# Bias rows of a graph network: four float32 rows, or twelve bf16 rows from an exact split

## The reference

```python
gi = x @ w_ih.T + b_ih
gh = h @ w_hh.T + b_hh
r = sigmoid(i_r + h_r); z = sigmoid(i_z + h_z)
n = tanh(i_n + r * h_n)
return (1.0 - z) * n + z * h
```

## Time and profile before

| | |
|---|---|
| three timed runs, us | 3788.97, 3793.4, 3793.51 (median 3793.4) |
| the profiled execution, us | 3787.5 |
| its span, first to last instruction, us | 3785.9 |
| mean granted TensorE clock | 0.836 |
| busy: PE, PEld | 2916.1 us (77%), 1831.7 us (48%) |
| busy: DVE, ACT, POOL | 2178.6 us (58%), 680.5 us (18%), 1629.3 us (43%) |

### The profile page before, as it was taken

The page is one execution under the profiler, slowest core; times in us unless marked ns, Lnnn a source line. Parts: engine busy times, 40 slices in busy tenths (PEclk is TensorE's granted clock), DMA queues, the critical chain, the costliest instruction groups (busy, mean ns, idle before and its releaser), DMA issues.

```text
span 3785.9 us, 53836 instructions
## 1 busy us (share of the span) xinstructions
PE 2916.1 (77%) x10862; PEld 1831.7 (48%) x10863; DVE 2178.6 (58%) x7167; ACT 680.5 (18%) x1768; POOL 1629.3 (43%) x1961
## 2 busy tenths in 40 slices
PE   2157777757778777777688877877777999999998
PEld 1133434435546444444476766642333666455754
DVE  5856666634443588888788888767775000543002
ACT  0012222200013222222100000015552000452000
POOL 0057777754320477777577777500000222001443
PEclk6578898889999888888677677657788999999999
DMA  2034322247641344443433333403332444003887
GB/s 95 33 77 112 108 101 101 101 129 199 192 125 44 84 106 107 107 106 106 74 99 103 102 103 104 77 2 124 126 126 88 146 139 142 1 1 106 276 268 231
DMA packets 317488, 423.25 MB, mean 112 GB/s; under 512 B 182634, under 2 KB 227888, under 8 KB 317014
## 3 DMA queue, kind: packets, MB, share of 16 engines
q0 software_dynamic: 105264, 324.88, 28.8%
q1 hardware_dynamic: 208024, 92.58, 9.4%
q10 hardware_dynamic: 3982, 3.24, 0.3%
HBM read 312.03 MB, written 112.79 MB: 112 GB/s over the span
## 4 chain that ended last, share of the span: by engine, by line
PE 43%; DVE 17%; DMA 13%; POOL 12%; issue 11%; ACT 2%; SPq 1%; DVEq 1%; POOLq 0%; ACTq 0%
PE PSA L846 14%; POOL G L450 7%; PE PSA L810 7%; DMA tab_m<-G,posi 6%; PE PSA L969 5%; PE PSA L833 5%; POOL tab_m L432 4%; DMA G<-tab_k,srci 4%; DVE S L1524 3%; PE PSA L1024 2%; DMA G<-tab_v,srci 2%; DVE S L1525 1%; DMA G<-tab_m 1%; PE PSA L923 1%; PE PSA L805 1%
## 5 line engine op out<-in xcount | busy, mean ns | idle before, releaser
L468 POOL DMA_DIRECT2D G<-tab_A x375 | 201.4, 538 | 1110.3 <-PE PSA L846 644.8
L432 POOL DMA_INDIRECT tab_m<-G,posi x448 | 436.4, 974 | 353.3 <-DVE G L1268 267.3
L450 POOL DMA_INDIRECT G<-tab_k,srci x448 | 426.2, 951 | 306.0 <-DMA tab_v<-KV 169.8
L450 POOL DMA_INDIRECT G<-tab_v,srci x448 | 439.7, 981 | 165.3 <-issue 96.6
L864 PE MATMUL PSA<-ident,oh 128*128 128x128 f32 x896 | 309.1, 345 | 232.2 <-DVE oh L1237 228.5
L969 PE MATMUL PSA<-work,oh 128*128 128x256 f32 x896 | 418.2, 560 | 46.9 <-DVE work L1452 32.0
L602 ACT COPY ohT<-PSA 128x128 f32<-128x128 f32 x896 | 237.5, 265 | 1062.6 <-PE PSA L864 1039.6
L1237 DVE TENSOR_SCALAR oh<-iota_f,dstl 128x128 f32<-128x128 f32 x1344 | 413.9, 309 | 5.5 <-DVE near L1373 0.5
L873 PE MATMUL PSA<-X,ohT 128*128 x896 | 349.4, 481 | 43.7 <-DVE G L1266 22.6
L923 PE MATMUL PSA<-Q,ohT 128*128 x896 | 365.6, 500 | 15.8 <-ACT ohT L602 8.0
L864 PEld LDWEIGHTS PSA<-ident,oh 128*128 128x128 f32 x896 | 143.8, 160 | 471.8 <-DVE oh L1237 448.0
(11 more groups left out here) (315 smaller groups left out, 4118.5 us busy)
## 6 DMA issues: line engine op xcount, KB each, us to landing
G<-tab_A POOLq DMA_DIRECT2D x375, 320.0 KB
tab_A<-G SPq DMA_DIRECT2D x125, 320.0 KB, 2.1
G<-tab_m SPq DMA_DIRECT2D x224, 129.0 KB, 2.6
G<-tab_m POOLq DMA_DIRECT2D x224, 129.0 KB
WT<-tab_m SPq DMA_DIRECT2D x544, 1.0 KB
rec<-tab_rec SPq DMA_DIRECT2D x448, 6.5 KB
tab_m<-G,posi POOLq DMA_INDIRECT x448
G<-tab_k,srci POOLq DMA_INDIRECT x448
```

Of the source, the lines that this page charges most:

```text
L432: pool.indirect_dma_start(tab_m[0:E, :], bass.IndirectOffsetOnAxis(ap=posi[:, t:t + 1], axis=0), G[:, t % GR, :MW], None, bounds_check=E - ...
L450: pool.indirect_dma_start(G[:, t % GR, :p.w], None, p.table, bass.IndirectOffsetOnAxis(ap=srci[:, t:t + 1], axis=0)).then_inc(p.rows[t % G ...
```

## The change

`brow` and `pick` are no longer tiles of their own; they lie in `oh` and `ohT`, which are free at the start, and the whole of `brow` is cleared by VectorE before `v_set`, for which ScalarE now waits before it loads the biases. After the two counts and a wait for the 22 weight turns, VectorE splits `brow` into three bf16 parts (each the rounded rest of the one before) in `Q`, makes `pick` bf16 and adds a fifth block, ones in rows 0 and 1. SyncE copies the three parts into the twelve rows of `bsplit` and three copies of the pick blocks into `bpick`: six transfers. Every bias product is then one bf16 product over all twelve rows.

```diff
-        brow = sb("brow", [4, 3 * D])
-        pick = sb("pick", [4, 4 * P])
+        bsplit = sb("bsplit", [12, 3 * D], BF16)
+        bpick = sb("bpick", [12, 5 * P], BF16)
+        bpart = Q[0:4, 0:3 * (3 * D) // 2].bitcast(BF16).rearrange("p (k n) -> p k n", k=3)
+        brest = Q[0:4, 2048:2048 + 3 * D]
+        bcast = Q[0:4, 4096:4096 + 5 * P // 2].bitcast(BF16)
...
+        brow = oh[:, :, :].rearrange("p r n -> p (r n)")[0:4, 0:3 * D]
+        pick = ohT[:, :, :].rearrange("p r n -> p (r n)")[0:4, :]
...
 (SyncE, after the input loads and before its wait for the places)
+            sp.wait_ge(s_("b_split"), 1)
+            for k in range(3):
+                sp.dma_start(bsplit[4 * k:4 * k + 4, :], bpart[:, k, :]).then_inc(s_("b_bias"), 16)
+                sp.dma_start(bpick[4 * k:4 * k + 4, :], bcast).then_inc(s_("b_bias"), 16)
...
 (ScalarE, before the bias loads)
+            act.wait_ge(v_set, 1)
...
 (TensorE, bias())
-                pe.matmul(ps, pick[0:k + 1, k * P:(k + 1) * P], brow[0:k + 1, BO[name] + off:BO[name] + off + n], start=True, stop=False)
+                pe.matmul(ps, bpick[:, k * P:(k + 1) * P], bsplit[:, BO[name] + off:BO[name] + off + n],
+                          start=True, stop=False)
...
 (TensorE, before stage n1)
+            pe.wait_ge(s_("b_bias"), 96)
...
 (TensorE, n3_gates)
-                pe.matmul(rz[:, 0:2 * D], ones[0:2, :], brow[0:2, 0:2 * D], start=True, stop=False)
+                pe.matmul(rz[:, 0:2 * D], bpick[:, 4 * P:5 * P], bsplit[:, 0:2 * D], start=True, stop=False)
...
 (VectorE, before v_set)
+            link(dve.memset(brow[:, :], 0.0))
...
 (VectorE, after both counts)
+            dve.wait_ge(wt_t, NWT)
+            link(dve.tensor_copy(bpart[:, 0, :], brow[:, :]))
+            link(dve.tensor_tensor(brest, brow[:, :], bpart[:, 0, :], ALU.subtract))
+            link(dve.tensor_copy(bpart[:, 1, :], brest))
+            link(dve.tensor_tensor(brest, brest, bpart[:, 1, :], ALU.subtract))
+            link(dve.tensor_copy(bpart[:, 2, :], brest))
+            link(dve.tensor_copy(bcast[:, 0:4 * P], pick[:, :]))
+            link(dve.tensor_tensor(bcast[:, 4 * P:5 * P], pick[:, 0:P], pick[:, P:2 * P], ALU.add))
+            dve.sem_inc(s_("b_split"), 1)
```

More of the change, by code:

```diff
@@ L190, in gnn_kernel @@
         assert 2 * D + DF + D1 == 3 * D
-        brow = sb("brow", [4, 3 * D])
-        pick = sb("pick", [4, 4 * P])
         bcols = sb("bcols", [P, 3])
+        bsplit = sb("bsplit", [12, 3 * D], BF16)
[3 more added lines that the diff above has]
+        bcast = Q[0:4, 4096:4096 + 5 * P // 2].bitcast(BF16)
+        assert NWT * D >= 4096 + 5 * P // 2
         wnat = Q[:, 0:NWT * D].rearrange("p (r n) -> p r n", n=D)
```

## The result

The changed kernel takes 3763.53 us (median of 4 runs, 3761.8 to 3766.05), the kernel before, on the same chip, 3793.45 us (4 runs, 3788.97 to 3797.13): ratio 0.9932, 95% interval 0.9918 to 0.9946, which leaves out 1. In another set of runs the ratio was 0.994 (0.9927 to 0.9953). The profiled execution after took 3762.92 us (span 3761.3), 24.6 us less than the one before.

A forecast was written before the change was run, and what follows sets the result against it. TensorE had the largest chain share (43%), but stages have different limits. Terms -11.2 -17.6 -0.45 +4.4 +0.5 = -24.4 us from 3787.5 gave 3763.1, plus 5.9: 3769.0 us; range 3756 to 3784.

The forecast's parts named there:

- n1: Stage of 25 tiles, one 256-column bias product each: 0.45 us saved per tile, 11.2 us in all (7.7 to 12.7).
- n3: Stage of 25 tiles, three bias products each: the loop over all engines limits turns to 8.30 us; 17.6 us saved.
- the last step: Adding 5.9 us, the timed median 3793.4 over the profiled execution, to 3763.1, giving 3769.0.
- The ends of the terms: The terms' lower and upper bounds taken together: -31 and -15 us, given as 3762 to 3778 us.
- The rival of 3744.6 us: The loop in n3 does not bind: n3 saves 42 us, sum -48.8 us; chance 0.04.
- The split: VectorE's splitting work after the second count at the start, all on the path: +4.4 us (3.5 to 6.2).
- the bound of 6.2: Upper bound of the split, if float32 to bf16 copies run at the tensor_tensor rate, each 0.44 us dearer.
- The first indirect transfer: Sign at the start: the stretch to the first indirect DMA becomes 5 us longer.
- Clearing of brow: VectorE's clearing before v_set, at the start: +0.5 us (0 to 0.87).
- fc2: One bias product between two others, for fc2: 0.45 us saved.
- price for the change of type: Rival: float32 to bf16 and back costs; at 0.45 us each the sum is -5.5, time 3787.9 us; chance 0.07.
- The clock in n3: Rival: TensorE's clock falls in n3 or n1, making the kernel slower, 3843 us if half the tiles; chance 0.05.

The follow-up runs named there:

- the table's two runs: One-column sigmoid behind each root of n3, loading the sigmoid's table early: on the changed kernel 3735.18 us (ratio 0.9883), on the kernel before 3778.09 us (0.9996).
- the doubled products: Changed kernel with each of the three bias products of a tile of n3 issued twice: 3764.82 us (one run).
- the kernel with nothing else: Kernel before plus only the start's additions (clearing of brow, ScalarE's wait, VectorE's split), parts unused, no SyncE transfers: 3784.71 us, ratio 1.0015.

## Why the prediction was right

*Verdict and time.* Faster, by 0.7%, and 3763.53 us lies in the range, 5.5 under the forecast of 3769.0. The sum of -24.4 us from the profiled execution's 3787.5 gave 3763.1; the profiled executions differ by 24.6. That these two meet to 0.2 us is luck: in this pair n1 shows 3.0 us less than its term and n3 0.7 more, and the untouched stretches give -2.7. What was off in the forecast is the last step: I added 5.9 us because the profiled execution before was that far below its median, and the one after was only 0.6 below. It is the scatter of single executions, not a term of the sum, and the medians' difference of 29.9 us carries it too (26.5 in the second set). The ends of the terms were also added wrong: they make -29 and -14, not -31 and -15, so the bounds were 3764 to 3779 us, and the measured time lies just below them, inside the range only by its widening. With the sizes measured in the traces the terms make -11.0 -18.3 +4.6 = -24.7 us; the intervals of both sets (20 to 31 and 18 to 28 us) hold that, and what else the medians' 29.9 contain is not shown.

*n1.* Predicted -11.2. The pair of traces shows -8.2, but in the one before the clock had risen by the first Q, K and V group and in the one after it had not. Three traces with the old products took 154.1, 154.3 and 154.1 us with slower groups, against 143.3 to 144.0 with the new: 10.6. Where the group took 2.86 on both sides it is 152.2 against 141.2: 11.0. The term was right in size, by two errors that cancel. At the lower clock, in the first two tiles, a product saves 0.83 us (1.15 before, 0.32 after), and I had credited 0.45. At the higher one it saves 0.41 instead of 0.45: I had put 0.05 to 0.06 for the unhidden load, and it is 0.10. That "what is saved there is made good later only if the clock rises as soon as now" was the right caution: the group took 2.6 us more in the trace after, most of the 3.0 by which the pair of traces misses the term.

*n3.* Predicted -17.6, measured -18.3 (2.9 before the first transpose of XS, 0.94 in the first turn, 22 x 0.658 = 14.5 in the turns). The step that mattered, that the loop and not TensorE holds the changed stage, is shown by the table's two runs and by the doubled products (one run). The turn was given as 8.30 and is 8.267; the first as 7.85, and it is 3242.10 - 3234.24 = 7.86. The rival of 3744.6 us, TensorE alone, would have needed turns of 7.25; with the loop shortened the turn is 7.364, the 0.11 above being the undersized products (2 x 0.04 + 0.05 = 0.13).

*The split.* Predicted +4.4, measured 4.57 to the memset of G, whole to 800 us, and 4.1 (0.8 to 10) in the times of the kernel with nothing else. The copies to bf16 took 0.55 us, near the 0.52 of the row they were taken from, so the bound of 6.2 did not come. That it counts in full held only for its place: 7 us later VectorE waits for TensorE, and there, in the trace, it costs nothing. I had priced the stretch as VectorE's throughout and not looked along it for a wait. The first indirect transfer, which the prediction named as a sign, came at 225.3 us instead of 221.5: 3.8 later for the 5 expected.

*Clearing of brow.* 0.70 us of VectorE, and the edge data came 0.15 later in the one pair; over all traces they came between 31.1 and 33.2 us, so 0.5 cannot be told from 0.

*fc2.* One product, in a stretch that differs by more than 0.4 us from run to run; left open.

*The rivals.* No price for the change of type was found: a bf16 product of the same height starts 0.11 us before the next one, its columns alone. The price found is for height, 0.1 us in the product and 0.2 around it. The prediction's rows had a hint of it, a float32 bias pass of few rows 0.05 to 0.08 us over a full one, but no term and no rival held that the products around it pay too. The clock in n3 stayed, 0.98, with TensorE waiting 0.67 us for XS in each turn.

## What to carry to other kernels

When an engine's work is cut in a pipelined stage, look at the end of the stage, where nothing fills it any more: the turn there (8.22 us) is what the others need and told the new turn to 0.05 us. Then ask what holds that loop, since it is where the next gain is: one column of sigmoid in ScalarE's idle time, worth nothing before, was worth 19 us after. Short preparations belong in a wait that the engine has already (shown here in the trace; in the times it is too small to tell), and small products between full ones are cheaper at full height, filled with zeros.

## What the runs showed of the hardware

A weight load of 12 rows between products of 128 rows starts with its product and not ahead of it, and so does the one behind it (1185.98 and 1186.19 us in the changed kernel): 0.30 us a place in n1 against zero-filled 128 rows, where both start 0.22 and 0.11 us ahead; between products of the same 12 rows nothing is lost (0.107 us for 256 bf16 columns, 0.42 ns a column).

The moment at which TensorE goes to its higher clock at the start of n1 varies, from 7.9 to 14.3 us after the first transposes in traces with the 12-row products: the same twelve products took from 2.86 to 5.49 us. A single pair of traces can be 2.6 us wrong on such a stage without any cause in the kernel.
